# Graph build of a four-layer graph network: count, weight and edge-bias columns from one product of 22 values, and batch sums in two pairs of PSUM banks

## The chip, the cores and the metric

One core of a Trainium2 chip runs the whole program. The metric is the device time of one execution in microseconds, as the median of runs. TensorE (PE in the profile) multiplies matrices, VectorE (DVE) and ScalarE (ACT) do elementwise work, GpSimd (POOL) gathers rows, SyncE (SP) issues most transfers.

## The reference

```
h = relu(layernorm(x));  x = x + attention(h, batch0, edge_index, edge_attr_16, ...)   # 32 graphs of 64 nodes, 8 heads
h = relu(layernorm(x));  x = x + gcn3(h, edge_index, ...)                              # normalised by in-degrees
h = relu(layernorm(x));  x = x + gcn1(h, edge_index, ...)                              # normalised by out-degrees
h = relu(layernorm(x));  x = x + relu(segment_sum((h @ W)[col] * edge_weight, row))
```

x has 2048 rows of 512. The 67584 edges (src, dst, 16 attributes, a weight) are sorted by dst. The kernel turns them once into dense matrices: `count` (how many edges between two nodes), the weights' sums (the last layer's matrix) and, for edges inside one graph of attention, the edge biases `edge_attr @ We + be` summed by pair of nodes. That work is the build. All later layers are dense products with these matrices.

## The kernel before

**Edge preparation** (to 50 us) finds where each node's edges begin and writes records of 11 fields to DRAM: src, dst, weight, 8 biases.

**The build** (50 to 419 us) handles edges in units of 64 partitions: one half of the partitions holds the edges of one destination node, the other half those of another. A tile is 128 such units; there are 8 tiles (t), each in 8 batches of 16 units, so 64 batches (n, with i = n modulo 8). For a tile, GpSimd gathers the records, TensorE turns them (`turn_fields`, L1154), ScalarE copies the fields to SBUF (`copy_fields`, L980), and VectorE makes keys (`prep_keys`, L779 to L790): the low 7 bits of src, and the tile of src. Values are split into two fp16 parts: ScalarE writes the high ones (`copy_part`, L991 for weights, L992 for biases), VectorE the rest (`residual`, L810, L811).

For a batch, `hots` on VectorE writes into one of two buffers: a comparison for counts and weights (L872, 32 columns per unit), one for the biases (L875, 16 columns twice), the one-hot rows of src (L877, 128 columns), the count columns times the weight parts (L887) and the tile columns times the bias parts (L894, 256 columns). It needs batch n-2 to be through TensorE. TensorE then (`build_pe`) sums the biases over the batch in one bank (L1255, 32 matmuls), and counts and weights of each unit in its own columns of four banks (L1266, L1267, 16 pairs). ScalarE copies both out (`copy_sums`: L1006 biases, L1013 counts, L1020 weights to a slab). TensorE turns the slab of batch n-4 (L1166), ScalarE scales it (L1001) and SyncE stores it.

**What runs beside it.** In the same batches the attention's projections are computed: TensorE turns h (L1175), ScalarE casts it to `h_t` (L1033), VectorE subtracts to get the low part (L819, inside `hots`, before the product), TensorE projects (L1201 in fp32 for the first slab, L1209, L1192), ScalarE copies results to `stage` (L1070, L1073, L1076) and SyncE stores them. `projections` fixes in which batch each piece stands: h is turned at batches 1, 6, 12, 17, 22, 28 and 33.

**Order and banks.** Each engine runs its own program in written order; semaphores join them. Turned fields, h pieces, projections and turned slabs share a ring of three PSUM banks (`work_slots`); a use waits until the third use before it has been read. In-degrees are one small matmul per tile (L1264) into spare columns of the sums' banks, added by VectorE in `evacuate` (L905), which waits for the slab copy.

In each ScalarE iteration n the order is: the batch's stage copies and casts, `copy_sums`, the scaled slab, and where i is 3 `copy_part` of the next tile.

## Time and profile before

| what | us |
|---|---|
| median of 3 runs | 1401.82 |
| lowest, highest | 1401.14, 1402.6 |
| span of the profiled execution | 1400.5 |
| PE, DVE, ACT busy in it | 1363.9, 886.7, 568.6 |

The profile comes from one execution. Its span runs from the first to the last instruction, without what lies around it. "Busy" of an engine is the time in which at least one of its instructions ran; matmuls are pipelined, so a row of 32 shows the last one's whole length after the start of the first. A start-to-start distance is therefore the better price of one instruction in a queue than its duration. `[1.96 <-DVE x_sb L894]` behind a row says that the engine had stood idle for 1.96 us and what ended it. Tile names come without buffer numbers; all one-hot columns lie in the memory of `x_sb`, all PSUM banks are `banks`.

### The profile page before, as it was taken

Reading aid. Unit: us, or ns where it says so; the run is one execution under the profiler, and the core shown is the slowest. Engines: PE = TensorE matmul, PEld = TensorE weight load, DVE = VectorE, ACT = ScalarE, POOL = GpSimd, SP = SyncE. Lnnn points to the kernel's source line nnn. Section 1 sums busy time; section 2 is a strip of 40 time slices with the busy share of each in tenths; the row PEclk is TensorE's granted clock in tenths of the full one; section 3 lists DMA queues with packets and bytes.
Section 4 is the critical chain, followed back from the end, with each engine's and each line's share of the span. In section 5 each row is a group of like instructions: output and inputs, shape, how many; then the busy total and the mean of one; then the engine's idle time right before and its main releaser. Section 6 shows DMA issues by size and latency. Waiting matters only on the chain.

```text
span 1400.5 us, 26694 instructions
## 1 busy us (share of the span) xinstructions
PE 1363.9 (97%) x11285; PEld 843.1 (60%) x11285; DVE 886.7 (63%) x1381; ACT 568.6 (41%) x980; POOL 88.0 (6%) x86
## 2 busy tenths in 40 slices
PE   9889999989998999999999999999999999999998
PEld 8779898989996655544444444454444445344443
DVE  7998998999988886567555666542354223532323
ACT  2666566656554457411142113221253224422312
POOL 3120010101002110000001000011100000000000
PEclk9999999999999999999999999999999999999999
DMA  9634344335348723000002000022210222563201
GB/s 335 227 114 148 137 138 137 126 119 177 120 146 286 238 94 108 1 31 1 0 0 61 0 0 1 1 59 77 68 40 29 73 71 78 200 212 104 91 0 60
DMA packets 71333, 136.92 MB, mean 98 GB/s; under 512 B 11908, under 2 KB 24324, under 8 KB 69798
## 3 DMA queue, kind: packets, MB, share of 16 engines
q1 hardware_dynamic: 68542, 123.98, 26.8%
q0 software_dynamic: 1280, 5.77, 1.5%
q10 hardware_dynamic: 1384, 5.38, 1.1%
q8 instruction: 92, 1.51, 0.5%
q14 instruction: 35, 0.29, 0.1%
HBM read 81.79 MB, written 53.32 MB: 96 GB/s over the span
## 4 chain that ended last, share of the span: by engine, by line
PE 83%; DVE 11%; ACT 2%; issue 2%; DMA 1%; POOL 0%; ACTq 0%; SPq 0%; DVEq 0%; POOLq 0%
PE banks L2305 31%; PE banks L2239 13%; PE banks L2369 12%; PE banks L1255 6%; PE banks L1655 4%; DVE x_sb L894 3%; PE banks L1192 3%; PE banks L1209 2%; PE banks L1266 2%; PE banks L1166 2%; DVE x_sb L877 1%; PE banks L2183 1%; PE banks L1625 1%; PE banks L298 1%; PE banks L1643 1%
## 5 line engine op out<-in xcount | busy, mean ns | idle before, releaser
L2305 PE MATMUL banks<-g,count 128*128 128x512 f16 x1024 | 227.6, 379 | 0.5 <-DVE tiles L2571 0.5
L2305 PE MATMUL banks<-count,g 128*128 128x512 f16 x1024 | 223.6, 379 | 0.0
L2239 PE MATMUL banks<-w_parts,h_parts 128*128 128x512 f16 x960 | 215.3, 379 | 1.7 <-DVE g L2520 1.4
L2305 PEld LDWEIGHTS banks<-count,g 128*128 128x128 f16 x1024 | 99.6, 98 | 118.0
L2305 PEld LDWEIGHTS banks<-g,count 128*128 128x128 f16 x1024 | 99.7, 98 | 113.6 <-DVE tiles L2571 1.0
L2369 PE MATMUL banks<-g,part 128*128 128x512 f16 x768 | 165.9, 379 | 0.0
L2239 PEld LDWEIGHTS banks<-w_parts,h_parts 128*128 128x128 f16 x960 | 91.2, 98 | 115.4 <-issue 11.4
L894 DVE TENSOR_TENSOR x_sb<-eb_parts,x_sb 128x4096 f16<-128x4096 f16 x64 | 146.0, 2281 | 0.0
L1255 PE MATMUL banks<-x_sb 128*128 128x128 f16 x2048 | 126.9, 221 | 11.9 <-DVE x_sb L894 11.8
L1255 PEld LDWEIGHTS banks<-x_sb 128*128 128x128 f16 x2048 | 120.9, 99 | 15.3 <-DVE x_sb L894 14.2
L2369 PEld LDWEIGHTS banks<-g,part 128*128 128x128 f16 x768 | 75.1, 98 | 90.6
L2652 DVE SCALAR_TENSOR_TENSOR part<-count,e_scale,part 128x1024 f16<-128x1024 f32 x29 | 37.2, 1284 | 105.9 <-ACT part L2136 105.9
L2110 ACT ACTIVATE h_gcn_t<-h_gcn_t,b_col,unscale 128x512 f32<-128x512 f32 x32 | 26.0, 813 | 169.2 <-DVE h_gcn_t L2563 169.2
L2136 ACT ACTIVATE part<-count,e_scale 128x1024 f16<-128x1024 f32 x29 | 33.3, 1148 | 110.9 <-PE banks L2369 110.9
L877 DVE TENSOR_TENSOR x_sb<-iota_src,keys 128x2048 f16<-128x2048 f16 x64 | 77.7, 1215 | 0.0
L2459 DVE TENSOR_TENSOR h_parts<-h_gcn_t,h_parts 128x512 f16<-128x512 f32 x48 | 39.6, 829 | 48.6 <-ACT h_parts L2019 48.6
L1266 PE MATMUL banks<-x_sb 128*128 128x64 f16 x1024 | 65.1, 190 | 0.0
L1267 PE MATMUL banks<-x_sb 128*128 128x32 f16 x1024 | 64.2, 178 | 0.0
L2520 DVE SCALAR_TENSOR_TENSOR g<-banks,g_scale,g 128x512 f16<-128x512 f32 x64 | 47.6, 747 | 22.1 <-ACT g L2042 22.0
L1266 PEld LDWEIGHTS banks<-x_sb 128*128 128x128 f16 x1024 | 60.8, 97 | 0.5
L1655 PE MATMUL banks<-wo_sb,att_t 128*128 128x512 f32 x128 | 58.7, 602 | 0.4 <-ACT att_t L1563 0.4
L1267 PEld LDWEIGHTS banks<-x_sb 128*128 128x128 f16 x1024 | 59.0, 96 | 0.1
(346 smaller groups left out, 1902.5 us busy)
## 6 DMA issues: line engine op xcount, KB each, us to landing
weight_dram<-w_new SPq DMA_DIRECT2D x60, 256.0 KB, 2.6
count<-weight_dram SPq DMA_DIRECT2D x29, 512.0 KB, 7.1
qk_dram<-stage SPq DMA_DIRECT2D x64, 128.0 KB, 2.6
tiles<-x_dram SPq DMA_DIRECT2D x32, 256.0 KB, 3.5
x_dram<-tiles SPq DMA_DIRECT2D x32, 256.0 KB, 2.8
count<-in_x SPq DMA_DIRECT2D x4, 1024.0 KB, 12.8
h<-in_x SPq DMA_DIRECT2D x16, 256.0 KB, 4.3
h_dram<-h_t SPq DMA_DIRECT2D x8, 512.0 KB, 3.3
```

Source lines behind the costliest of these rows:

```text
L877: dve.tensor_tensor(m.hot_src[:, z].rearrange("p g (c two) -> p g c two", two=2), keep.iota_src[:].rearrange("p (c two) -> p c two", two=2 ...
L894: dve.tensor_tensor(m.hot_eb[:, z].rearrange("p g (t c) -> p g t c", t=NT), values, tiles, ALU.mult).then_inc(s["hots"], 1)
L1192: mm = pe.matmul(out, m.h_slab[slab % 2][:, zh, k, tile * P:(tile + 1) * P], keep.wq[:, zw, k, c * SCOLS:(c + 1) * SCOLS], start=n == 0, s ...
L1255: mm = pe.matmul(m.bias_ps[:, 0:NT * H], m.hot_src[:, z, g], parts[:, part], start=g == part == 0, stop=g == BATCH - 1 and part == 1)
L1266: pe.matmul(m.cw_ps[:, g, 0:2 * CCOLS], m.hot_src[:, z, g], m.hot_cw[:, z, g, 0:2 * CCOLS], start=True, stop=False)
L1267: mm = pe.matmul(m.cw_ps[:, g, CCOLS:2 * CCOLS], m.hot_src[:, z, g], m.hot_cw[:, z, g, 2 * CCOLS:CW], start=False, stop=True)
L1655: mm = pe.matmul(m.wo_ps[:, t % 2], m.att_t[:, k, :], keep.wo[:, k, :], start=k == 0, stop=k == KT - 1)
L2239: mm = pe.matmul(out, m.h_parts[:, slot, zh, k], m.w_parts[:, zw, k], start=n == 0 and layer != 3, stop=n == len(passes) - 1)
L2305: mm = pe.matmul(m.agg_ps[:, b], lhs, rhs, start=i == 0 and z == 0, stop=i == NT - 1 and z == 1)
L2369: mm = pe.matmul(m.banks[:, b], m.part[:, n % 3, z, b * P:(b + 1) * P], m.g[:, q, gz], start=q == 0 and (z, gz) == (0, 0), stop=q == NT - ...
L2459: dve.tensor_tensor(out, source, hi, ALU.subtract).then_inc(s["lo"], 1)
L2520: dve.scalar_tensor_tensor(lo, result, scale, hi, ALU.mult, ALU.subtract).then_inc(s["glo"], 1)
```

## The change

A unit now has one row of 22 values in fp16: 8 high bias parts, 8 low ones, the weight's low part for each half of the partitions, its high part for each half, and a one for each half (zero in the other half). One comparison makes 16 tile columns twice (L873 after the change), and one product (L889) multiplies all 11 pairs of values with these 32 contiguous columns, 352 columns per unit in place of 256 plus 64. The comparison L872 and the product L887 are gone. The zeros and ones are written before the first keys (`mark_halves`); the weight times its scale, zero in the other half, is made with the keys into `w_half`. `copy_part` stands one batch later and waits for the keys. The sums of counts and weights take 64 columns per unit, so a batch fills two banks, and two batches alternate between two pairs. The in-degree matmul takes a bank of the ring.

```diff
@@ -564 @@ build_memory
-    n_src, n_eb, n_cw, n_tile = (2 * BATCH * c for c in (P, NT * HP, CW, 2 * NT))
-    m.eb_parts = place("eb_parts", [P, 2, P, HP], F16, AT_EB)
+    n_src, n_val, n_tile = (2 * BATCH * c for c in (P, NT * VALUES, 2 * NT))
+    m.parts = place("parts0", [P, P, VALUES], F16, AT_EB)[:], place("parts1", [P, P, VALUES], F16, AT_REST + 15360)[:]
     m.w_slab = place("w_slab", [P, 2, 4, BATCH * CCOLS], F32, AT_SLAB)
     m.fields = place("fields", [P, FIELDS, P], F32, AT_REST + 5632)
     m.h_t = place("h0_t", [P, 2, KT, SCOLS], F16, AT_REST + 11264)
-    m.keys = place("keys", [P, 2, 2, P, 2], BF16, AT_REST + 15360)
-    m.ints = place("ints", [P, 3, P], I32, AT_REST + 17408)
-    m.w_parts = place("w_parts", [P, 2, P, 2, 2], F16, AT_REST + 18944)
+    m.ints = place("ints", [P, 2, P], I32, AT_EB + 5632)
+    m.w_half = m.ints[:].rearrange("p two u -> p (two u)").bitcast(F32).rearrange("p (u half) -> p u half", half=2)
+    m.src_keys = [place(f"src_key{z}", [P, P, 2], BF16, AT_EB + 6656 + 512 * z)[:] for z in range(2)]
+    m.tile_keys = place("tile_key0", [P, P, 2], BF16, AT_EB + 7680)[:], place("tile_key1", [P, P, 2], BF16, AT_REST + 23040)[:]
...
-    m.cw_ps = keep.banks[:, WORK:7].rearrange("p b (g c) -> p (b g) c", c=P)
-    m.deg_ps = m.cw_ps[0:2 * GTILES, 0:GROUPS, CW:P]
+    m.cw_ps = keep.banks[:, WORK:7].rearrange("p (z b) (g c) -> p z (b g) c", z=2, c=2 * CCOLS)
@@ -716 @@ work_slots
+        if i == 0:
+            use(("deg", t), ("added", t + 1 if first_round else n + 1))
@@ -780 @@ prep_keys
-        dve.tensor_scalar(m.ints[:, 1], m.ints[:, 0], P - 1, None, ALU.bitwise_and)
-        dve.tensor_scalar(m.ints[:, 2], m.ints[:, 0], 7, None, ALU.logical_shift_right).then_inc(s["dve"], 1)
+        dve.tensor_scalar(m.ints[:, 1], m.ints[:, 0], P - 1, None, ALU.bitwise_and).then_inc(s["dve"], 1)
+        k += 1
+        dve.wait_ge(s["dve"], k)
+        dve.tensor_scalar(m.ints[:, 0], m.ints[:, 0], 7, None, ALU.logical_shift_right).then_inc(s["dve"], 1)
         k += 1
         dve.wait_ge(s["dve"], k)
         dve.tensor_scalar(keep.match[:], dlocal, 0.0, None, ALU.is_equal)
         twice = [P, P, 2]
-        dve.tensor_copy(m.keys[:, z, 0], m.ints[:, 1].unsqueeze(2).to_broadcast(twice))
-        dve.scalar_tensor_tensor(m.keys[:, z, 1], dlocal.unsqueeze(2).to_broadcast(twice), float(P),
-                                 m.ints[:, 2].unsqueeze(2).to_broadcast(twice), ALU.mult, ALU.add).then_inc(s["keyed"], 1)
+        dve.tensor_copy(m.src_keys[z], m.ints[:, 1].unsqueeze(2).to_broadcast(twice))
+        settle(dve.scalar_tensor_tensor(m.tile_keys[z], dlocal.unsqueeze(2).to_broadcast(twice), float(P),
+                                 m.ints[:, 0].unsqueeze(2).to_broadcast(twice), ALU.mult, ALU.add))
+        dve.tensor_tensor(m.w_half, m.fields[:, 2, :].unsqueeze(2).to_broadcast(twice),
+                          keep.half_scale[:].unsqueeze(1).to_broadcast(twice), ALU.mult).then_inc(s["keyed"], 1)
@@ -804 @@ residual
-        dve.scalar_tensor_tensor(m.w_parts[:, z, units, 1], weight, keep.scale[:, 1:2], m.w_parts[:, z, units, 0], ALU.mult, ALU.subtract)
-        dve.scalar_tensor_tensor(m.eb_parts[:, z, units, H:HP], biases, keep.scale[:, 0:1], m.eb_parts[:, z, units, 0:H],
+        dve.tensor_tensor(parts[:, units, W_LO:W_LO + 2], m.w_half[:, units], parts[:, units, W_HI:W_HI + 2], ALU.subtract)
+        dve.scalar_tensor_tensor(parts[:, units, H:HP], biases, keep.scale[:, 0:1], parts[:, units, 0:H],
@@ -861 @@ hots
-        dve.tensor_tensor(cw[:, :, 0:CCOLS].rearrange("p g (c two) -> p g c two", two=2),
-                          keep.iota_cnt[:].rearrange("p (c two) -> p c two", two=2).unsqueeze(1).to_broadcast([P, BATCH, NT, 2]),
-                          key(1, CCOLS), ALU.is_equal).then_inc(s["dve"], 1)
-        dve.tensor_tensor(m.hot_tile[:, z], keep.iota_tile[:].unsqueeze(1).to_broadcast([P, BATCH, NT, 2]),
-                          m.keys[:, ts, 1, units].unsqueeze(2).to_broadcast([P, BATCH, NT, 2]), ALU.is_equal).then_inc(s["dve"], 1)
+        dve.tensor_tensor(m.hot_tile[:, z].rearrange("p g (t two) -> p g t two", two=2), keep.iota_tile[:].unsqueeze(1).to_broadcast([P, BATCH, NT, 2]),
+                          m.tile_keys[ts][:, units].unsqueeze(2).to_broadcast([P, BATCH, NT, 2]), ALU.is_equal).then_inc(s["dve"], 1)
         dve.tensor_tensor(m.hot_src[:, z].rearrange("p g (c two) -> p g c two", two=2),
                           keep.iota_src[:].rearrange("p (c two) -> p c two", two=2).unsqueeze(1).to_broadcast([P, BATCH, P // 2, 2]),
-                          key(0, P), ALU.is_equal)
+                          m.src_keys[ts][:, units].unsqueeze(2).to_broadcast([P, BATCH, P // 2, 2]), ALU.is_equal)
         nonlocal k
-        k += 2
+        k += 1
         dve.wait_ge(s["dve"], k)
         if n == 0:
             residual(0)
         if units.start in [u.start for u in unit_parts(t, first_round)]:
             dve.wait_ge(s["parts"], part_count(t, 1 if units.start else 0, first_round))
-        dve.tensor_tensor(cw[:, :, CCOLS:CW].rearrange("p g (z c two) -> p g z c two", z=2, two=2),
-                          cw[:, :, 0:CCOLS].rearrange("p g (c two) -> p g c two", two=2).unsqueeze(2).to_broadcast([P, BATCH, 2, NT, 2]),
-                          m.w_parts[:, ts, units].unsqueeze(3).to_broadcast([P, BATCH, 2, NT, 2]), ALU.mult)
         for tile in turned:
             h_low(tile)
-        tiles = m.hot_tile[:, z].rearrange("p g t two -> p (g t) two").unsqueeze(2).to_broadcast([P, BATCH * NT, H, 2])
-        values = m.eb_parts[:, ts, units].unsqueeze(2).to_broadcast([P, BATCH, NT, HP])
-        dve.tensor_tensor(m.hot_eb[:, z].rearrange("p g (t c) -> p g t c", t=NT), values, tiles, ALU.mult).then_inc(s["hots"], 1)
+        tiles = m.hot_tile[:, z].unsqueeze(2).to_broadcast([P, BATCH, PAIRS, 2 * NT])
+        values = m.parts[ts][:, units].rearrange("p u (c two) -> p (u c) two", two=2).unsqueeze(2).to_broadcast([P, BATCH * PAIRS, NT, 2])
+        dve.tensor_tensor(m.hot_val[:, z].rearrange("p g (c t) -> p g c t", c=PAIRS), values, tiles, ALU.mult).then_inc(s["hots"], 1)

+    def mark_halves():
+
+        for parts in m.parts:
+            settle(dve.memset(parts[:, :, HP:VALUES], 0.0))
+            for half in range(2):
+                dve.memset(parts[half * WHALF:(half + 1) * WHALF, :, ONE + half], 1.0)
+        if first_round:
+            dve.wait_ge(keep.prep["pool"], 12)
+            dve.tensor_scalar(keep.half_scale[:], keep.half_of[:, GTILES - 1:2 * GTILES:GTILES], keep.scale[:, 1:2], None, ALU.mult)
@@ -896 @@ evacuate
-            dve.wait_ge(s["slab"], n + 1)
-            part = CPT // GROUPS
-            op = dve.tensor_tensor(keep.deg[:].rearrange("q b (g c) -> q b g c", c=part), m.deg_ps.rearrange("q g (c b) -> q b g c", c=part),
-                                   keep.deg[:].rearrange("q b (g c) -> q b g c", c=part), ALU.add)
+            bank, _ = uses["deg", n // NBATCH]
+            dve.wait_ge(s["batch"], n + 1)
+            op = dve.tensor_tensor(keep.deg[:], m.work_ps[0:2 * GTILES, bank, 0:P].rearrange("q (c b) -> q b c", c=CPT), keep.deg[:], ALU.add)
@@ -930 @@ build_dve
     pieces = projections(first_round)
+    mark_halves()
     if first_round:
         other_norms()
     prep_keys(0)
@@ -983 @@ copy_part
-        act.activation(m.w_parts[:, z, units, 0], weight, ACT.Copy, scale=keep.scale[:, 1:2])
-        act.activation(m.eb_parts[:, z, units, 0:H], biases, ACT.Copy, scale=keep.scale[:, 0:1]).then_inc(s["copied"], 1)
+        act.wait_ge(s["keyed"], t + 1)
+        act.copy(parts[:, units, W_HI:W_HI + 2], m.w_half[:, units])
+        act.activation(parts[:, units, 0:H], biases, ACT.Copy, scale=keep.scale[:, 0:1]).then_inc(s["copied"], 1)
@@ -1003 @@ copy_sums
-            act.copy(to_count, m.cw_ps[:, :, 0:CCOLS].rearrange("p (c b) (h s) -> p s c b h", c=GROUPS, h=2))
+            act.copy(to_count, sums[:, :, CCOLS:2 * CCOLS].rearrange("p (c b) (s h) -> p s c b h", c=GROUPS, h=2))
...
-        slab = m.w_slab[:, q % 2, n % 4].rearrange("p (b c) -> p b c", b=BATCH)
-        act.copy(slab, m.cw_ps[:, :, CCOLS:2 * CCOLS]).then_inc(s["slab"], 1)
+        slab = m.w_slab[:, q % 2, n % 4].rearrange("p (b h s) -> p b h s", h=2, s=NT)
+        act.copy(slab, sums[:, :, 0:CCOLS].rearrange("p b (s h) -> p b h s", h=2)).then_inc(s["slab"], 1)
@@ -1121 @@ build_act
-        if t + 1 < GTILES and i == 3:
+        if t + 1 < GTILES and i == 4:
             copy_part(t + 1)
@@ -1250 @@ build_pe
-            parts = m.hot_eb[:, z, g].rearrange("p (t two h) -> p two t h", two=2, h=H)
             for part in range(2):
-                mm = pe.matmul(m.bias_ps[:, 0:NT * H], m.hot_src[:, z, g], parts[:, part], start=g == part == 0,
+                mm = pe.matmul(m.bias_ps[:, 0:EB_COLS], m.hot_src[:, z, g], m.hot_val[:, z, g, part * EB_COLS:(part + 1) * EB_COLS], start=g == part == 0,
                                stop=g == BATCH - 1 and part == 1)
         mm.then_inc(s["bias_done"], 1)
         if t + 1 < GTILES and i == 3:
             turn_fields(t + 1)
-        if n:
-            pe.wait_ge(s["slab"], n)
-            pe.wait_ge(s["added"], added(n - 1))
+        if n >= 2:
+            pe.wait_ge(s["slab"], n - 1)
+            if not first_round:
+                pe.wait_ge(s["added"], n - 1)
         if i == 0:
-            pe.matmul(m.deg_ps, keep.half_of[:, GTILES - 1 - t:3 * GTILES - 1 - t], keep.match[:], start=True, stop=True)
+            bank, free = uses["deg", t]
+            if free:
+                pe.wait_ge(s[free[0]], free[1])
+            pe.matmul(m.work_ps[0:2 * GTILES, bank, 0:P], keep.half_of[:, GTILES - 1 - t:3 * GTILES - 1 - t], keep.match[:], start=True, stop=True)
         for g in range(BATCH):
-            pe.matmul(m.cw_ps[:, g, 0:2 * CCOLS], m.hot_src[:, z, g], m.hot_cw[:, z, g, 0:2 * CCOLS], start=True, stop=False)
-            mm = pe.matmul(m.cw_ps[:, g, CCOLS:2 * CCOLS], m.hot_src[:, z, g], m.hot_cw[:, z, g, 2 * CCOLS:CW], start=False, stop=True)
+            pe.matmul(m.cw_ps[:, z, g], m.hot_src[:, z, g], m.hot_val[:, z, g, W_HI * NT:VALUES * NT], start=True, stop=False)
+            mm = pe.matmul(m.cw_ps[:, z, g, 0:CCOLS], m.hot_src[:, z, g], m.hot_val[:, z, g, W_LO * NT:W_HI * NT], start=False, stop=True)
```

ScalarE, from batch 11 to the projections of batch 13. Before:

```order
L1020 COPY w_slab<-banks 128x512
L1001 ACTIVATE w_new<-banks,scale 128x512 [waits first_store1,first_chunk]
L991 ACTIVATE w_parts<-fields,scale 128x128x2 [waits first_hots,first_turned]
L992 ACTIVATE eb_parts<-fields,scale 128x128x8
L1073 ACTIVATE stage<-banks,bk_col,w_small 128x256 [waits first_out_p3,first_proj]
L1033 CAST h_t<-banks 128x4x128 [waits first_out_h,first_h_turned] x2
L1006 COPY bias<-banks 128x16x8 [waits first_bias_done]
L1013 CAST count<-banks 128x64x8 [waits first_batch]
```

And after, from the same place on:

```order
L1032 COPY w_slab<-banks 128x512
L1012 ACTIVATE w_new<-banks,scale 128x512 [waits first_store1,first_chunk]
L1085 ACTIVATE stage<-banks,bk_col,w_small 128x256 [waits first_out_p3,first_proj]
L1045 CAST h_t<-banks 128x4x128 [waits first_out_h,first_h_turned] x2
L1017 COPY bias<-banks 128x128 [waits first_bias_done]
L1025 CAST count<-banks 128x64x8 [waits first_batch]
L1032 COPY w_slab<-banks 128x512 [waits first_chunk]
L1012 ACTIVATE w_new<-banks,scale 128x512 [waits first_store0,first_chunk]
L1002 CAST parts_79<-ints 128x128x2 [waits first_keyed,first_hots,first_turned]
L1003 ACTIVATE parts_79<-fields,scale 128x128x8
L1082 ACTIVATE stage<-banks,bq_col,w_small 128x256 [waits first_out_p0,first_proj]
```

The two value copies moved behind the casts of h and behind batch 12's sums, and the first of them waits for the keys.

VectorE at the start of the build (`parts_79` and `parts_80` are the two value tiles). Before:

```order
L523 TENSOR_SCALAR scale<-scale 128x4 [waits prep_dve]
L1421 TENSOR_LOAD rounds [waits counted]
L798 RECIPROCAL rstd<-rstd 128x12 [waits prep_std]
L801 SCALAR_TENSOR_TENSOR shift<-stats_119,rstd 128x12 [waits first_dve]
L779 CAST ints<-fields 128x128 [waits first_turned]
```

After:

```order
L521 TENSOR_SCALAR scale<-scale 128x4 [waits prep_dve]
L1435 TENSOR_LOAD rounds [waits counted]
L894 MEMSET parts_79 128x128x3
L896 MEMSET parts_79 64x128 [waits first_dve]
L896 MEMSET parts_79 64x128
L894 MEMSET parts_80 128x128x3
L896 MEMSET parts_80 64x128 [waits first_dve]
L896 MEMSET parts_80 64x128
L899 TENSOR_SCALAR half_scale<-half_of,scale 128x2 [waits prep_pool]
L804 RECIPROCAL rstd<-rstd 128x12 [waits prep_std]
L807 SCALAR_TENSOR_TENSOR shift<-stats_122,rstd 128x12 [waits first_dve]
L781 CAST ints<-fields 128x128 [waits first_turned]
```

Seven instructions stand ahead of the norms and the first keys that did not stand there.

## Rows read from the trace of the kernel before

**Rows 1.** The page's first part: busy us, share of span, instructions.
```profile
PE 1363.9 (97%) x11285; PEld 843.1 (60%) x11285; DVE 886.7 (63%) x1381; ACT 568.6 (41%) x980; POOL 88.0 (6%) x86
```
**Rows 2.** Busy time by stretch: length, PE, PEld, DVE, ACT, POOL, granted clock, DMA share, GB/s.
```profile
100.00:145.00 45.00, 42.43 (x685) 40.05 (x683) 40.59 (x52) 29.55 (x59) 2.94 (x2) 1.00 0.49 156
```
**Rows 3.** Waits of PE in 50-180, 180-300, 300-420: us, times, longest.
```profile
PE banks L1255 <- DVE x_sb L894: 5.8, 4, 2.0
...
PE banks L1255 <- DVE x_sb L894: 4.9, 2, 2.9
...
PE banks L1255 <- DVE x_sb L894: 1.2, 1, 1.2
```
**Rows 4.** Timeline of DVE, one batch: start, duration, line, tiles, count, [idle before].
```profile
110.16 0.43 DVE L872 TENSOR_TENSOR x_sb<-iota_cnt,keys 128x512 f16<-128x512 f16 x1
...
110.83 1.23 DVE L877 TENSOR_TENSOR x_sb<-iota_src,keys 128x2048 f16<-128x2048 f16 x1
111.97 0.70 DVE L887 TENSOR_TENSOR x_sb<-x_sb,w_parts 128x1024 f16<-128x1024 f16 x1
112.57 2.29 DVE L894 TENSOR_TENSOR x_sb<-eb_parts,x_sb 128x4096 f16<-128x4096 f16 x1
115.74 0.28 DVE L905 TENSOR_TENSOR deg<-banks,deg 16x128 f32<-16x128 f32 x1 [0.87 <-ACT w_slab L1020]
```
**Rows 5.** Timeline of DVE at the program's start: a memset.
```profile
0.94 0.27 DVE L424 MEMSET bins<- 128x256 f32 x1 [0.94 <-PEq L2801]
```
**Rows 6.** Timelines of DVE, ACT and PE at the start of the build.
```profile
50.48 0.23 DVE L779 CAST ints<-fields 128x128 int32<-128x128 f32 x1 [0.28 <-ACT fields L980]
...
51.41 0.35 ACT L991 ACTIVATE w_parts<-fields,scale 128x64 f16<-128x64 f32 x1
...
54.17 0.82 ACT L1070 ACTIVATE stage<-banks,bq_col 128x256 f32<-128x256 f32 x2
...
55.78 3.62 PE L1201 MATMUL banks<-h_first,w_slab 128*128 128x256 f32 x16
...
59.65 1.95 PE L1255 MATMUL banks<-x_sb 128*128 128x128 f16 x32
```
**Rows 7.** Timeline of DVE in the keys of a tile.
```profile
139.72 0.22 DVE L784 TENSOR_SCALAR ints<-ints 128x128 int32<-128x128 int32 x1
139.98 0.23 DVE L787 TENSOR_SCALAR match<-fields 128x128 f16<-128x128 f32 x1
...
140.32 0.42 DVE L790 SCALAR_TENSOR_TENSOR keys<-fields,ints 128x256 bf16<-128x256 f32 x1
```
**Rows 8.** Timeline of PE at batch 7's bias product.
```profile
105.70 1.51 PE L1255 MATMUL banks<-x_sb 128*128 128x128 f16 x24 [0.64 <-DVE x_sb L894]
```
**Rows 9.** Timelines of DVE, ACT and PE, batches 12 to 15.
```profile
130.84 0.42 DVE L872 TENSOR_TENSOR x_sb<-iota_cnt,keys 128x512 f16<-128x512 f16 x1 [1.00 <-PE banks L1267]
...
132.78 2.11 ACT L992 ACTIVATE eb_parts<-fields,scale 128x1024 f16<-128x1024 f32 x1
...
135.85 1.29 DVE L819 TENSOR_TENSOR h_t<-banks,h_t 128x512 f16<-128x512 f32 x2 [2.51 <-ACT h_t L1033]
...
152.34 1.85 PE L1255 MATMUL banks<-x_sb 128*128 128x128 f16 x30 [1.96 <-DVE x_sb L894]
```
**Rows 10.** Timelines of ACT and PE, batches 20 to 23.
```profile
185.93 0.70 ACT L1001 ACTIVATE w_new<-banks,scale 128x512 f32<-128x512 f32 x1
...
193.10 1.06 ACT L1033 CAST h_t<-banks 128x512 f16<-128x512 f32 x2
...
198.07 0.34 PE L1255 MATMUL banks<-x_sb 128*128 128x128 f16 x3
```
**Rows 11.** PE after a wait: its row, then stretches (length, busy, granted clock, DMA).
```profile
244.70 1.51 PE L1255 MATMUL banks<-x_sb 128*128 128x128 f16 x24 [1.96 <-DVE x_sb L894]
...
246.00:248.00 2.00, 2.00 (x40) 0.52 0.00 0
248.00:250.00 2.00, 2.00 (x21) 0.63 0.00 0
```

49 lines of the change are left out of this document (25 added, 24 removed).

## The prediction

> **What bounds the kernel now.** I read in this order: busy time by engine, the build in stretches, who waited for whom, then single rows. TensorE is busy for 1363.9 of 1400.5 us [rows 1]. The change touches the build alone, 64 batches between about 50 and 419 us. There VectorE is nearly as full, 40.59 of 45 us against TensorE's 42.43 between 100 and 145 us [rows 2]. Two chains run side by side, tied by two buffers of one-hot columns. The waits say which is late: TensorE's bias product waited for VectorE's value product L894 for 5.8 us before 180, 4.9 until 300, 1.2 after [rows 3]. Nothing on TensorE waited for the batch sums to be copied (no row names L1266). So VectorE sets the pace in the first 55 us of the build and in short stretches later, TensorE elsewhere. VectorE time moves the end only on those stretches, and 11.9 us of such waits is all that there is.
>
> **The VectorE batch.** From start to start L872 and L875 take 0.67 us together, L877 1.14, L887 0.60; L894 lasts 2.29, of which 0.09 overlaps the next, so 4.61 a batch [rows 4]. L872 (0.34) and L887 go: -0.94. L894 grows from 4096 to 5632 columns. Its slope comes from two rows of one form: 2048 columns take 1.22 us, 4096 take 2.29, so 0.522 ns a column, and 1536 more are 0.80 us. Net -0.14 us a batch, 9 us in all, most of it where TensorE is late anyway. The new product repeats a pair of columns 16 times against 32 contiguous ones; L877 too repeats a pair against a contiguous row, and runs at L894's slope, so I take that slope. The other end is one column a cycle, as in fp32: L790's 256 columns in 0.42 us [rows 7], 0.15 of it fixed (1.22 less 2048x0.522), are 1.05 ns a column, +3 us a batch. The Trainium skill, "Advanced Engine Details and Errata", section 2x-1p Requirements, asks 16-bit types, a 4-byte aligned start and unit step innermost for two elements a cycle; rows of 22 values, 44 bytes, keep that, so by the page too the fast form stands.
>
> **TensorE's own work** I cost at nothing. The bias products lose a strided operand. 32 of them take 1.95 us [rows 6]; with a tail of 0.2 that is 56 ns each for 128 columns, 2.7 ns over the 53.3 of the full clock. If that were all the stride, 2048 of them would give 5.5 us back. I take none, since every row of matmuls has some such excess; it is a reason for the low end. The sums keep 64 and 32 columns per unit. The second pair of banks relaxes a wait that is in no row: nothing.
>
> **Start (+1.8).** VectorE now clears and marks both value tiles right before the first keys. A clear is 384 words wide; 256 words took 0.27 us [rows 5], 0.05 of it overlap, so 0.33, plus 0.1 for the wait on it (L784 to L787, across a wait, is 0.26; L787 to L790, two starts without one, 0.34 [rows 7], so 0.17 each). Four marks of 128 are 0.12 each, the scaling 0.15: 1.5 us, of which 0.28 fits in the wait that L779 had [rows 6]: +1.2. The keys get two waits (0.1 each) and a product of 256 columns in fp32 like L790 (0.34 to the next start): 0.54, with its rounding taken as +0.6 per tile of eight batches. ScalarE's first copy waits for those keys (51.41 before, 53.9 after), and with it its queue: the stage copies at 54.17. TensorE's fourth projection needs the first stage copy's bank, at 57.2 instead of 55.8; bias 0 goes from 59.65 to about 61.5 [rows 6]. VectorE ends batch 1's columns 1.5 us late (1.2+0.6-2x0.14) and has no idle time before 115 us: -0.14 for each of six batches, +0.6 for the second tile's keys, +0.5 for a cast of h that ScalarE delivers late at batch 6, since its value copy now stands behind the keys. +1.8 at the bias product of 105.70 [rows 8]. From there TensorE is late by itself and carries that on. Ends: +0.5 if ScalarE's lateness stays hidden and the marks are cheaper, +3.5 if it is not.
>
> **The value copy one batch later.** L991 and L992 hold ScalarE 2.4 us once a tile (the larger is 2.11 [rows 9]), after batch 3 of the tile; now after batch 4 and behind the keys. Take T as the moment when VectorE begins the columns of batch 5 of a tile: 130.84 after 1.00 us of waiting for TensorE [rows 9], and so in four more tiles, at 179.16, 223.21, 272.10 and 317.24. Keys are ready at T+4.47+2.0=T+6.5; ScalarE is at that place of its queue at T+7.5 where two projections precede (185.93 and 0.6 more [rows 10]), so it mostly doesn't wait and ends at T+10. TensorE needs its banks at T+12. Nothing is lost there.
> Two tiles win, batches 12 and 28 (T=130.84 and 223.21), where h is turned at batch 4 of the tile. Before, the casts stood behind the value copy: VectorE waited 2.51 us for them, until T+5.0, and TensorE at the end 1.96 us for VectorE [rows 9]. Now the casts end at T+3.5, both subtractions T+4.1, the product (3.0) T+7.1, keys T+9.1, batch 6's columns (4.47) T+13.6, residuals (2.3) T+15.9, batch 7's columns T+20.4, and its bias product starts at T+20.5 instead of T+21.5 (152.34). TensorE alone would be there at T+19.4. So -1.0 each, -2.0 for both, not 2.5 each, since VectorE stays the late one.
> One tile loses, batch 22 (T=179.16). ScalarE's value copy ends at T+9.9; then come two stage copies, two relus, the copies of batch 21 (their bank free at T+14.25), one stage copy and the casts, which end at T+16.3 instead of T+15.0 (193.10 and 1.06). VectorE's subtractions, then the product, put the bias product of batch 23 at T+19.6 instead of T+18.9 (198.07 [rows 10]): +0.7. The tile at 272 turns no h there; its keys cost +0.6 and three batches give back 0.4: +0.2.
>
> **The in-degree count** moves to the ring of three work banks. VectorE's wait for it was for the slab copy (0.87 us at 115.74 [rows 4]) and is now for the batch itself, about 1.1 us earlier; VectorE runs into TensorE again at the next T in every tile, so nothing. The ring's next user of that bank comes after the next batch's bias product, where the old wait stood too: nothing.
>
> **Sum.** +1.8 -2.0 +0.7 +0.2 = +0.7 on a span of 1400.5: 1401.2. The median of the runs, 1401.82, is 1.3 above that span; the same on top gives **1402.5 us**.
>
> **Rivals.** *The clock.* After the 1.96 us wait at 244.70 TensorE's granted clock read 0.52 and 0.63 for two times 2 us [rows 11], so for about 1.7 us the work of full clock (2.4 GHz) was withheld at half of it; the equal wait at 152.34 left it at full. I price that at 1.5. With the wait halved the drop may go: 1402.5-1.5=1401.0, still no change; with a start at its low end (-1.3) and no loss at batch 22 (-0.7) it is 1399.0, at the edge of faster. The Trainium skill, "TensorE: Matmul & The Clock Gate", section What's actually happening, says that the activity window runs free of the kernel; by that a shift of 1.8 us alone could place or remove a drop, which fits that equal waits ended differently here. *ScalarE becomes the late engine (slower).* Place: behind the keys at batch 4 of each tile. TensorE's turns of h at batch 6 need a bank that ScalarE frees after the value copy, three copies later; there I get 2.4 us of new wait, counted as covered because VectorE is late too. It decides where the value copy ends later than T+12, that is, if keys or copies are 2 us slower than taken. Then the start costs 3.5, batch 22 2.0, the two gains fall to 0.5 each, and one new drop of the clock comes on top (1.5): 1401.8+3.5-1.0+2.0+0.2+1.5=1408. *The product loses the fast form:* 64 times 3 us, about 1590. *VectorE's saving counts everywhere (faster):* the start costs nothing, both gains stand, and the waits [rows 3] shrink by 0.14 for each of some 20 batches ahead of them: 1401.8-2.0-2.8=1397.
>
> **Chances.** A measurement of this kernel can tell about 0.2%, 2.8 us. The forecast has 0.48, the clock's 1401.0 another 0.14, its edge and VectorE's saving everywhere 0.17, ScalarE late 0.18, the slow product 0.03. So faster 0.17, same 0.62, slower 0.21. Range: 1397.8 to 1406.5; it reaches most of the way to both rivals and leaves out the slow product.
>
> **What would show it.** The new product at 3.05 to 3.15 us; batch starts 4.47 us apart where VectorE is full; first keys near 51.8 and bias 0 near 61.5; the 2.5 us wait for the casts at batches 12 and 28 down to about 1.5; a wait of ScalarE for keys of 2 us in the first tile, little later; TensorE's waits for the product no fewer than before in the first 60 us. Wrong would be: a product off 3.1 us, ScalarE copies over 0.7 us because their source in PSUM is now strided, bias products under 55 ns, or a second tile in which TensorE waits for ScalarE.

## The result and the profile after

The changed kernel takes **1403.65 us** (median of 20 runs, 1402.18 to 1405.15) against 1401.81 (20 runs on the same chips): a ratio of 1.0016, 95% interval 1.001 to 1.0022. That is within 0.2% and inside the range; the point, 1402.5, was 1.15 low. Its profiled execution spans 1402.1 us, 1.6 more than before. The kernel before scatters from 1399 to 1404 and the medians of single experiments are good to about 1 us, so below I follow each effect in the traces and name the median beside it.

Busy time first, the page's first part (busy us, share of span, instructions), which answers [rows 1]:

```profile
PE 1364.0 (97%) x11285; PEld 841.3 (60%) x11285; DVE 883.6 (63%) x1268; ACT 568.6 (41%) x980; POOL 85.6 (6%) x84
```

VectorE has 113 instructions fewer and is busy for only 3.1 us less, and none of that is seen at the end. TensorE's waits for the value product, by the groups of PE in the three stretches 50 to 180, 180 to 300, 300 to 420 (count, busy, mean ns, idle before them and for whom), against [rows 3]:

```profile
L1265 PE MATMUL banks<-x_sb 128*128 128x128 f16 x640 | 39.0, 219 | 3.6 <-DVE x_sb L889 2.7 <-ACT bias L1017 0.9
...
L1265 PE MATMUL banks<-x_sb 128*128 128x128 f16 x675 | 42.2, 222 | 4.2 <-DVE x_sb L889 4.2
...
L1265 PE MATMUL banks<-x_sb 128*128 128x128 f16 x736 | 44.9, 219 | 1.0 <-DVE x_sb L889 1.0
```

These waits fell from 11.9 to 7.9 us, and yet the kernel is no faster. To see where the time went, take the start of the bias product of each batch after (L1265) less the same before (L1255). This offset is +4.4 us at batch 0, +4.2 at batches 7 to 12, +3.25 at batches 15 to 21, +3.6 at 23 to 28, +2.7 at 31, +1.3 at 32 to 37, +1.1 from 41 to the last; the rest of the 1.6 comes behind the build. So against this trace everything is lost in the first 5 us of the build and most of it won back later. VectorE's timeline there (start, duration, line, tiles, count, [idle before]), against [rows 6]:

```profile
49.81 0.17 DVE L521 TENSOR_SCALAR scale<-scale 128x4 int32<-128x4 int32 x1
50.53 0.38 DVE L894 MEMSET parts<- 128x384 uint32 x1 [0.55 <-issue]
51.43 0.17 DVE L896 MEMSET parts<- 64x128 f16 x1 [0.53 <-DVE parts L894]
52.11 0.17 DVE L896 MEMSET parts<- 64x128 f16 x1 [0.51 <-issue]
52.40 0.38 DVE L894 MEMSET parts<- 128x384 uint32 x1
53.30 0.17 DVE L896 MEMSET parts<- 64x128 f16 x1 [0.52 <-DVE parts L894]
53.97 0.17 DVE L896 MEMSET parts<- 64x128 f16 x1 [0.51 <-issue]
54.15 0.23 DVE L899 TENSOR_SCALAR half_scale<-half_of,scale 128x2 f32<-128x2 f16 x1
...
54.63 0.22 DVE L781 CAST ints<-fields 128x128 int32<-128x128 f32 x1
```

A mark (L896, a fill of one column with 1.0) is busy for 0.17 us, but 0.51 to 0.53 us of idle time stand before each of the four. From the first clear to the start of the scaling it is 3.6 us where I had 1.5 with the scaling in it. The last step of the scaling factor, L521 here and L523 before, also starts 0.65 later (49.81 against 49.16), ahead of all that the change touches; I call this the drift and take it off: 4.20 - 0.65 = **3.55 us** is what the start costs against this one trace of the kernel before. That trace is an early one: four more profiles below have the start of the kernel before unchanged (the two with the later copy alone and two built on it), and their offsets at batch 2 are 0.3, 1.2, 1.2 and 2.1. The drift explains this only in part (it is 0.3, -0.55, 1.1 and 0.6); the section on the hardware comes back to it.

The places of the two gains, VectorE's subtraction of h at batch 12 and TensorE's bias products of batches 15, 23 and 31, against [rows 9 to 11]:

```profile
138.04 1.29 DVE L824 TENSOR_TENSOR h_t<-banks,h_t 128x512 f16<-128x512 f32 x2 [1.44 <-ACT h_t L1045]
...
155.59 1.62 PE L1265 MATMUL banks<-x_sb 128*128 128x128 f16 x26 [0.90 <-DVE x_sb L889]
...
201.68 1.51 PE L1265 MATMUL banks<-x_sb 128*128 128x128 f16 x24 [0.17 <-DVE x_sb L889]
...
247.37 1.85 PE L1265 MATMUL banks<-x_sb 128*128 128x128 f16 x30 [0.90 <-DVE x_sb L889]
```

VectorE's wait for the casts is 1.44 instead of 2.51, TensorE's two waits 0.90 instead of 1.96. And TensorE's clock after the wait at 247.37 (length, busy of each engine, granted clock, DMA share, GB/s):

```profile
248.00:250.00 2.00, 2.00 (x55) 2.00 (x53) 2.00 (x2) 0.39 (x1) 0.00 (x0) 1.00 0.21 66
250.00:252.00 2.00, 2.00 (x26) 1.84 (x22) 2.00 (x2) 1.67 (x3) 0.00 (x0) 1.00 0.00 0
```

It stays at full clock (2.4 GHz) where [rows 11] read 0.52 and 0.63. The offset falls by 1.39 us between batches 31 and 32: that is this drop's price.

The single product and the keys, grouped over the build's VectorE work (count, busy us, mean ns, idle before):

```profile
L889 DVE TENSOR_TENSOR x_sb<-parts,x_sb 128x5632 f16<-128x5632 f16 x64 | 197.2, 3081 | 0.0
...
L796 DVE TENSOR_TENSOR ints<-fields,half_scale 128x256 f32<-128x256 f32 x8 | 3.4, 424 | 0.3
```

### The profile page after: what moved, and what is told of

Its sections match the earlier page's. It is cut to its first block, busy times and chain, and to the rows that moved or that the text cites. A ratio compares the mean times of both kernels' runs of the same rounds, so it can differ in the third digit from the quotient of the medians.

```text
span 1402.1 us, 26531 instructions
## 1 busy us (share of the span) xinstructions
PE 1364.0 (97%) x11285; PEld 841.3 (60%) x11285; DVE 883.6 (63%) x1268; ACT 568.6 (41%) x980; POOL 85.6 (6%) x84
## 4 chain that ended last, share of the span: by engine, by line
PE 83%; DVE 12%; ACT 2%; issue 2%; DMA 1%; DVEq 0%; ACTq 0%
PE banks L2319 31%; PE banks L2253 13%; PE banks L2383 11%; PE banks L1265 6%; DVE x_sb L889 5%; PE banks L1669 3%; PE banks L1206 3%; PE banks L1223 2%; PE banks L1280 2%; PE banks L1180 2%; DVE x_sb L875 1%; PE banks L2197 1%; PE banks L1639 1%; PE banks L296 1%; PE banks L1657 1%
## 5 line engine op out<-in xcount | busy, mean ns | idle before, releaser
L889 DVE TENSOR_TENSOR x_sb<-parts,x_sb 128x5632 f16<-128x5632 f16 x64 | 197.2, 3081 | 0.0
L2253 PEld LDWEIGHTS banks<-w_parts,h_parts 128*128 128x128 f16 x960 | 91.1, 98 | 115.1 <-issue 11.9
L1265 PE MATMUL banks<-x_sb 128*128 128x128 f16 x2048 | 125.8, 220 | 8.7 <-DVE x_sb L889 7.9
L1265 PEld LDWEIGHTS banks<-x_sb 128*128 128x128 f16 x2048 | 119.9, 98 | 12.2 <-DVE x_sb L889 11.0
L875 DVE TENSOR_TENSOR x_sb<-iota_src,src_key 128x2048 f16<-128x2048 f16 x64 | 77.7, 1215 | 0.0
```

The costliest lines, as they stand in the source:

```text
L875: dve.tensor_tensor(m.hot_src[:, z].rearrange("p g (c two) -> p g c two", two=2), keep.iota_src[:].rearrange("p (c two) -> p c two", two=2 ...
L889: dve.tensor_tensor(m.hot_val[:, z].rearrange("p g (c t) -> p g c t", c=PAIRS), values, tiles, ALU.mult).then_inc(s["hots"], 1)
L1265: mm = pe.matmul(m.bias_ps[:, 0:EB_COLS], m.hot_src[:, z, g], m.hot_val[:, z, g, part * EB_COLS:(part + 1) * EB_COLS], start=g == part == ...
L2253: mm = pe.matmul(out, m.h_parts[:, slot, zh, k], m.w_parts[:, zw, k], start=n == 0 and layer != 3, stop=n == len(passes) - 1)
```

## The experiments

Theory A: the change loses its time in the marks at the start, gains by the later value copy (with the clock), and the single product itself saves nothing. Rivals: ScalarE, held up behind the keys, is what is late at the start (B); the clock moves by itself (C).

### The later copy alone, on the kernel before

```diff
-        if t + 1 < GTILES and i == 3:
+        if t + 1 < GTILES and i == 4:
             copy_part(t + 1)
```

> The kernel before, with only ScalarE's value copy (L991 and L992) moved from behind batch 3 of a tile to behind batch 4; two products, the count comparison and the old banks stay. Theory A (the change's gains come from the moved copy, its losses from the marks and keys at the start): batches 12 and 28 gain 1.5 each (VectorE's wait for the casts of h goes from 2.5 to about 1.0 us), the drop of the clock at 244.70 goes too (1.4), batch 22 loses 0.3, the start is unchanged: 1401.8 - 3.0 - 1.4 + 0.3 = 1397.7, ratio 0.997. Theory B (the copy is neutral, and what the changed kernel gained there came from the shorter VectorE batch): within 0.5 of 1401.8. Theory C (the clock's drop came away by the shift of the time alone, free of the wait): 1401.8 - 2.7 = 1399.1 with 0.5 for two stretches of 2 us still in the clock's row near 246.

Measured: **1395.87 us** (5 runs, 1395.67 to 1396.24), ratio 0.9958, interval 0.9944 to 0.9971. It is ahead of both kernels, clear of the scatter. At batch 12 and at batch 15's bias product:

```profile
134.10 1.29 DVE L819 TENSOR_TENSOR h_t<-banks,h_t 128x512 f16<-128x512 f32 x2 [0.43 <-ACT h_t L1033]
...
150.58 0.62 PE L1255 MATMUL banks<-x_sb 128*128 128x128 f16 x8 [0.59 <-DVE x_sb L894]
```

The wait for the casts went from 2.51 to 0.43. Against the kernel before, the offset falls by 2.09 at batch 12 and 2.11 at batch 28, not 1.5: 1.37 each is TensorE's wait before the last product of the tile, and 0.72 I had not seen, a wait of TensorE's projections for VectorE's subtraction (0.56 us at 137.28 before) that goes as well. The drop at 246 goes (1.39), and so does the one at 290, for 0.95 more. These are 6.5; less a drift of 0.3 and 0.1 lost at batch 22, the last batch comes 6.1 earlier. Here is the clock from the end of TensorE's wait of 2.96 us, at 285.34, on:

```profile
284.00:286.00 2.00, 0.66 (x12) 0.66 (x13) 2.00 (x3) 0.00 (x0) 0.00 (x0) 1.00 0.05 17
286.00:288.00 2.00, 2.00 (x56) 2.00 (x54) 2.00 (x4) 0.38 (x1) 0.00 (x0) 1.00 0.27 37
```

Theory A holds in kind and was too low in size; the neutral copy is out. That the clock goes by itself is not excluded by this one kernel, in which both waits and times changed.

> The same kernel as the one before with the value copy behind batch 4, once more, for the clock. Its first profile had a wait of 2.96 us of TensorE at 285 and no drop, where the kernel before had 2.94 and a drop. If the program's own waits decide on the drop, this one is again without drops in the build, and the time within 0.5 of 1395.9. If it is the time at which the wait falls against something free of the kernel, drops may come in the build in one of the runs, and with each about 1.4 us: up to 1398.7.

The same kernel once more: 1397.0 us (5 runs, 1395.41 to 1398.24), ratio 0.9962, interval 0.9949 to 0.9975. Its profile again has no drop between batch 0 and the end of the build, and every wait for the product repeats within 0.05 us. But its bias 0 is 0.97 us later than in the first profile and all that follows 0.9, with the same program and a scaling factor that is ready 0.8 earlier: TensorE's clock came back to full at 52.2 instead of 48.8. One of the five runs, at 1398.24, is high enough to hold a drop; the spread does not say where.

### The later copy undone, in the changed kernel

First the order alone: ScalarE copies the bias fields ahead of its wait for the keys.

```diff
-        act.wait_ge(s["keyed"], t + 1)
-        act.copy(parts[:, units, W_HI:W_HI + 2], m.w_half[:, units])
-        act.activation(parts[:, units, 0:H], biases, ACT.Copy, scale=keep.scale[:, 0:1]).then_inc(s["copied"], 1)
+        act.activation(parts[:, units, 0:H], biases, ACT.Copy, scale=keep.scale[:, 0:1])
...
+    def copy_weight(t, piece=0):
...
+        act.wait_ge(s["keyed"], t + 1)
+        act.copy(parts[:, units, W_HI:W_HI + 2], m.w_half[:, units]).then_inc(s["copied"], 1)
...
+            copy_weight(t + 1)
```

> The changed kernel, with ScalarE's value copy (bias fields, L1003) issued ahead of the wait for the keys and only the small copy of the weights (L1002) behind it; same places in the queue. In the first tile ScalarE waits 3.99 us for the keys, and 2.63, 2.3 and 1.1 us later. Theory A (VectorE's marks and keys are what is late; ScalarE follows): VectorE's residual starts at most 0.6 us earlier and the stage copies 2.3 us earlier, TensorE's wait of 1.69 us for the stage copy goes, and bias 0 moves by 0.5: 1403.65 - 0.5 = 1403.1. Rival (ScalarE held up behind the keys is the late engine): 2 us or more off the start and 1 more at the second tile: 1400.6.

Measured: 1403.54 us (11 runs, 1402.03 to 1404.16), no change from 1403.65. ScalarE did get ahead: TensorE's projection at the start waited 0.89 for the stage copy instead of 1.69, and without the drifts bias 0 came 1.85 earlier, not the 0.5 that I expected. But then TensorE waited for VectorE and had lost all of it by batch 1, first for w_small, then for the in-degrees' bank:

```profile
68.23 1.99 PE L1222 MATMUL banks<-h_first,w_slab 128*128 128x256 f32 x8 [0.77 <-DVE w_small L846]
71.27 1.09 PE L1196 MATMUL banks<-ident,h 128*128 128x128 f32 x8 [1.04 <-DVE deg L916]
```

At batch 7 the offset less its own drift (L521 at 50.16, so 1.0) is 3.57, against 3.55 with ScalarE behind the keys. So ScalarE's 4 us of waiting cost nothing at the end; theory B is out, and my -0.5 with it.

Then the bias fields' copy back behind batch 3 (`i == 3`), with the small copy of the weights still behind batch 4:

> The changed kernel, with the bias fields' copy (L1003) back behind batch 3 of a tile as before the change, and only the small copy of the weights behind the keys after batch 4. It undoes the move by one batch. Theory A (the move gave 0.95 at each of batches 12 and 28 and 1.4 by the clock): against the version that only swaps the two copies 1.9 lost plus up to 1.4: 1403.1 + 2.6 = 1405.7, with VectorE's wait for the casts of h back at 2.5 us. Rival (the move is neutral): 1403.1 and that wait at 1.4.

Measured: 1408.93 us (5 runs, 1408.13 to 1410.83), 5.4 above the version with the order alone; I had said 2.6.

```profile
139.19 1.29 DVE L824 TENSOR_TENSOR h_t<-banks,h_t 128x512 f16<-128x512 f32 x2 [3.11 <-ACT h_t L1049]
...
156.73 1.46 PE L1273 MATMUL banks<-x_sb 128*128 128x128 f16 x23 [2.05 <-DVE x_sb L889]
```

The wait for the casts is 3.11. From trace to trace the move is worth 1.68 at each of batches 12 and 28 and 1.39 by the clock, 4.75 together. The error was in taking 0.95 for the move: 0.95 is what was left of it after the rest of the change had taken its part. With the copy early, the changed kernel is **0.7 behind the kernel before** at each of the two batches (offset 3.68 before batch 12 and 4.39 from batch 15 on).

### The marks

Two copies out of a constant tile in place of two clears and four marks:

```diff
-        for parts in m.parts:
-            settle(dve.memset(parts[:, :, HP:VALUES], 0.0))
-            for half in range(2):
-                dve.memset(parts[half * WHALF:(half + 1) * WHALF, :, ONE + half], 1.0)
         if first_round:
             dve.wait_ge(keep.prep["pool"], 12)
+        for parts in m.parts:
+            settle(dve.tensor_copy(parts[:, :, ONE:VALUES], keep.half_of[:, GTILES - 1:2 * GTILES:GTILES].unsqueeze(1).to_broadcast([P, P, 2])))
...
```

> The changed kernel, with the two clears and four marks of mark_halves (3.6 us of VectorE from the first to the last) replaced by two copies of 256 columns out of half_of, about 0.35 us each. Theory A: first keys 2.9 us earlier (51.8 instead of 54.6), bias 0 and all that follows 2.5 to 2.9 earlier, since VectorE has no idle time until 115 us: 1403.65 - 2.7 = 1401.0. Rival (the late start is TensorE's and ScalarE's own, the marks hide behind them): bias 0 moves by less than 1 us and the total by less than 0.7: 1403.0.

Measured: 1401.4 us (11 runs, 1399.35 to 1402.62), 2.25 less than the changed kernel.

```profile
49.49 0.63 DVE L896 COPY parts<-half_of 128x256 f16<-128x256 f16 x2 [0.43 <-issue]
...
50.71 0.23 DVE L781 CAST ints<-fields 128x128 int32<-128x128 f32 x1
...
58.85 1.22 DVE L830 TENSOR_TENSOR h_t<-h_first,h_t 128x1024 f16<-128x1024 f32 x1 [0.63 <-ACT h_t L1115]
```

The start costs 1.30 now (offset 1.03 at batch 7, drift -0.27) instead of 3.55: the clears and marks are 2.25 of it, by trace and by median alike. VectorE's keys are 3.0 earlier when each drift is taken off; 0.63 of that VectorE gives back in a wait for h that it did not have. Theory A, 0.4 off in size.

The reverse, the same clears and marks put into the kernel before, ahead of the first keys:

```diff
...
+        for z in range(2):
+            parts = m.hot_eb[:, z].rearrange("p g c -> p (g c)")[:, 0:22 * P].rearrange("p (u c) -> p u c", c=22)
+            settle(dve.memset(parts[:, :, 16:22], 0.0))
+            for half in range(2):
+                dve.memset(parts[half * WHALF:(half + 1) * WHALF, :, 20 + half], 1.0)
```

> The kernel before, with nothing changed but two clears and four marks of the changed kernel's shapes added ahead of the first keys (into the one-hot columns' memory, which the first batch overwrites). Theory A (the marks are the larger part of the late start, and nothing downstream gives them back): they take 3.6 us of VectorE as in the changed kernel, 0.28 fits in a wait, TensorE's own chain covers about 0.7 more: bias 0 2.6 later, 1401.9 + 2.6 = 1404.5. Rival (as I had sized them: 1.5 us less 0.28): 1403.1. Rival (hidden): 1402.0.

Measured: 1404.02 us (12 runs, 1402.76 to 1405.66), ratio 1.0018, interval 1.0009 to 1.0027. That is 2.4 above the kernel before on the same chip, nearer to the 2.6 of theory A than to the 1.2 that I had sized first. The six fills take as long as in the changed kernel. Bias 0 is only 2.56 later; at batch 2 TensorE waits 3.21 us for VectorE's product, and from there to batch 31 the offset is 4.32, 3.48 without its drift of 0.84. So the whole start cost of the changed kernel by the same reckoning (3.55) is there with nothing changed but the marks. The last batch comes only 2.7 later, since the drop at 246 is missing from this trace too:

```profile
249.03 1.18 PE L1268 MATMUL banks<-x_sb 128*128 128x128 f16 x18 [1.95 <-DVE x_sb L894]
...
250.00:252.00 2.00, 2.00 (x52) 2.00 (x50) 2.00 (x3) 0.50 (x2) 0.00 (x0) 1.00 0.00 0
252.00:254.00 2.00, 2.00 (x21) 1.80 (x20) 2.00 (x3) 1.80 (x4) 0.00 (x0) 1.00 0.00 0
```

This is the same wait as in [rows 11], 1.95 against 1.96 us, and no drop. So a halved wait is not needed to lose the drop. What differs here is the time at which the wait falls; that this is the cause is not shown.

What makes a mark dear? 14 small fills and copies in front of the first keys of the kernel before:

```diff
+        for half in range(2):
+            dve.memset(parts[half * WHALF:(half + 1) * WHALF, :, 2 + half], 0.0)
+        for j in range(2):
+            dve.memset(parts[:, :, 4 + j], 1.0)
+        for j in range(2):
+            dve.memset(parts[:, :, 6 + j], 0.0)
...
+        for j in range(2):
+            dve.memset(flat[:, 128 * j:128 * j + 128], 1.0)
...
```

> The kernel before, with 14 small operations of VectorE ahead of the first keys: clears and fills of 128 columns strided by 22 on 64 and on 128 partitions with 0.0 and with 1.0, fills of pairs, fills of 128 contiguous columns, copies of a pair and of one column from half_of. In the changed kernel each fill of 1.0 on 64 partitions had 0.51 to 0.53 us of idle time before it, and one of two wide clears 0.55. If the value 1.0 causes it, the fills of 1.0 on 128 partitions and the contiguous ones show it and the clears don't; if 64 partitions cause it, the clears and copies on 64 partitions show it and none on 128; if the stride causes it, all but the contiguous ones show it; if it is any fill, copies alone are without it. The time is some 4 to 8 us above the kernel before.

It took 1407.27 us (one run). VectorE's timeline, in order: single columns on 64 partitions with 0.0, on 128 with 1.0, on 128 with 0.0; then pairs of columns with 1.0 (two), contiguous ones (two), copies of pairs (two), copies of single columns on 64 partitions (two):

```profile
51.57 0.17 DVE L945 MEMSET x_sb<- 64x128 f16 x1 [0.51 <-issue]
52.25 0.17 DVE L947 MEMSET x_sb<- 128x128 f16 x1 [0.51 <-issue]
52.82 0.17 DVE L947 MEMSET x_sb<- 128x128 f16 x1 [0.41 <-issue]
53.39 0.17 DVE L949 MEMSET x_sb<- 128x128 f16 x1 [0.41 <-issue]
53.97 0.17 DVE L949 MEMSET x_sb<- 128x128 f16 x1 [0.41 <-issue]
54.12 0.55 DVE L951 MEMSET x_sb<- 128x256 f16 x2
54.64 0.30 DVE L953 MEMSET x_sb<- 128x128 f16 x2
54.87 0.63 DVE L955 COPY x_sb<-half_of 128x256 f16<-128x256 f16 x2
55.42 0.75 DVE L957 COPY x_sb<-half_of 64x128 f16<-64x128 f16 x2
```

Neither the value nor the number of partitions matters much: every fill of single 16-bit elements at a stride of 44 bytes has 0.4 to 0.5 us before it, fills of pairs and of contiguous columns have none. Twice as many elements in pairs are done in 0.27 us each, less than half the time of the single ones. The idle time is not a tail of the fill before: the first fill of pairs starts 0.15 us after the last single one, with none, and in the changed kernel so do the second clear and the scaling behind a mark. It goes with the single fill that follows it. Nor is the stride alone enough: the two copies of single 16-bit columns have no idle time and take 0.75 us together. The dear form is a fill of single 16-bit elements; what the engine does in that time the records can't say.

Last, the same 128 places as one 32-bit word each:

```diff
-            settle(dve.memset(parts[:, :, HP:VALUES], 0.0))
+            words = parts.rearrange("p u c -> p (u c)").bitcast(I32).rearrange("p (u w) -> p u w", w=PAIRS)[:, :, ONE // 2]
             for half in range(2):
-                dve.memset(parts[half * WHALF:(half + 1) * WHALF, :, ONE + half], 1.0)
+                op = dve.memset(words[half * WHALF:(half + 1) * WHALF], 15360 << 16 * half)
+            settle(op)
```

> The changed kernel, with the two wide clears left out (their other columns are written anyway) and each of the four marks written as one 32-bit word per unit (one half 1.0, the other 0.0) in place of one 16-bit column: the same 64 partitions, the same 128 places 44 bytes apart. In the probe, fills of single 16-bit columns had 0.41 to 0.51 us of idle time before each, whatever the value and the partitions, fills of pairs and of contiguous columns none. Theory D (it is the lone 16-bit element): marks 0.15 each without idle time, with one wait on them 0.8 us in all instead of 3.6, VectorE's first keys 2.8 earlier than in the changed kernel against the end of the scaling chain, 2.2 kept at the end as with the copied marks: 1401.4. Rival (it is the lone element of any size, at a stride): about 0.5 idle before each, 2.7 us in all, and 1402.8.

```profile
50.28 0.17 DVE L896 MEMSET parts<- 64x128 int32 x1 [0.58 <-issue]
50.61 0.17 DVE L896 MEMSET parts<- 64x128 int32 x1 [0.17 <-issue]
50.96 0.17 DVE L896 MEMSET parts<- 64x128 int32 x1 [0.19 <-DVE parts L896]
51.28 0.17 DVE L896 MEMSET parts<- 64x128 int32 x1 [0.16 <-issue]
```

1401.16 us (11 runs, 1398.58 to 1402.6), 0.2 from what was expected. 0.33 us from one to the next instead of 0.68: mostly the 16-bit element. Against the end of the scaling chain the keys come 2.4 earlier, not 2.8, and the offset without drift is 1.32 at batch 7, so 2.2 are kept, as with the copied marks (the two wide clears are gone here too). The idle time of 0.16 to 0.19 that is left was not expected with it, so theory D is right in the main and not in full. Some idle time before the first operation (0.58) stands in all these versions of the changed kernel (0.55, 0.43).

### The single product

> The kernel before with the value copy behind batch 4 (1395.9 us) and one more edit: where h is turned, the weights' product L887 (0.60 from start to start) stands behind VectorE's subtractions for h instead of ahead of them, so that it no longer runs while VectorE would wait for the casts. It is a model of what the single product does, which holds the weights' part too and comes as a whole behind the casts. Theory A (the single product lengthens what stands between the casts and the bias product): batches 12 and 28 lose 0.6 each, and 22 up to 0.6, so 1397.3 to 1397.7. Rival (it costs nothing, since VectorE catches up): within 0.4 of 1395.9.

```diff
+        for tile in turned:
+            h_low(tile)
         dve.tensor_tensor(cw[:, :, CCOLS:CW].rearrange("p g (z c two) -> p g z c two", z=2, two=2),
                           cw[:, :, 0:CCOLS].rearrange("p g (c two) -> p g c two", two=2).unsqueeze(2).to_broadcast([P, BATCH, 2, NT, 2]),
                           m.w_parts[:, ts, units].unsqueeze(3).to_broadcast([P, BATCH, 2, NT, 2]), ALU.mult)
-        for tile in turned:
-            h_low(tile)
```

Measured: 1398.92 us (11 runs, 1397.85 to 1401.3), more than the 1397.3 to 1397.7 expected and 3.0 and 1.9 above the two sets of runs of the same kernel with L887 ahead. At batches 12 and 15:

```profile
135.06 1.29 DVE L819 TENSOR_TENSOR h_t<-banks,h_t 128x512 f16<-128x512 f32 x2 [1.10 <-ACT h_t L1033]
...
152.15 1.07 PE L1255 MATMUL banks<-x_sb 128*128 128x128 f16 x16 [1.28 <-DVE x_sb L894]
```

VectorE waits 0.67 longer for the casts, since it has 0.6 less to do meanwhile, and TensorE waits 1.28 instead of 0.59. The offset grows by 0.69 at batch 12, 0.49 at 22 and 0.70 at 28, 1.9 in all; 0.95 more comes with the clock, whose drop at 290 is back. So work that stood in a wait and is moved behind it costs its full length. The single product does just this with the weights' part of itself; that it pays for it in the same way is argued from this model and fits the 0.7 a batch by which the changed kernel with the early copy is behind.

Two versions more make the price of the product's surroundings visible. In both, the product of weights and halves (L796) is gone, and the high and low weight columns are each written in two operations of one column per unit:

```diff
...
-        act.wait_ge(s["keyed"], t + 1)
-        act.copy(parts[:, units, W_HI:W_HI + 2], m.w_half[:, units])
+        for half in range(2):
+            act.activation(parts[:, units, W_HI + half], m.fields[:, 2, units], ACT.Copy, scale=keep.half_scale[:, half:half + 1])
```

> The version with the copied marks, in which the product of weights and halves (L796, 0.42 us of VectorE per tile) is gone: ScalarE makes the two high weight columns itself with a scale per partition, two operations of 128 columns in place of one of 256, VectorE subtracts them in two operations in place of one, and ScalarE's value copy no longer waits for the keys. Theory A (VectorE's work per tile counts where VectorE is late; ScalarE's wait hardly): start 0.4 earlier, batches 12 and 28 0.3 each: 1401.4 - 1.0 = 1400.4. Rival (ScalarE behind the keys is what costs): 2 us or more: 1399.2 or less.

Measured: 1402.45 us (12 runs, 1399.79 to 1404.93), 1.05 more than the version with copied marks, where 1.0 less was expected. The two were measured on different chips, and 1.05 is about what such medians are good to; the traces say more clearly that it lost (its last batch is 1.8 later, drifts taken off). ScalarE and then VectorE in one tile of this version, then ScalarE in the one with copied marks:

```profile
139.00 1.47 ACT L1001 ACTIVATE parts<-fields,half_scale 128x128 f16<-128x128 f32 x2
139.93 2.11 ACT L1002 ACTIVATE parts<-fields,scale 128x1024 f16<-128x1024 f32 x1
...
145.29 1.36 DVE L814 SCALAR_TENSOR_TENSOR parts<-fields,half_scale,parts 128x128 f16<-128x128 f32 x2
146.25 2.06 DVE L816 SCALAR_TENSOR_TENSOR parts<-fields,scale,parts 128x1024 f16<-128x1024 f32 x1
```
```profile
141.24 0.43 ACT L1001 CAST parts<-ints 128x256 f16<-128x256 f32 x1 [2.34 <-DVE ints L796]
141.56 2.14 ACT L1002 ACTIVATE parts<-fields,scale 128x1024 f16<-128x1024 f32 x1
```

The two operations of 128 single 16-bit elements overlap, so their price is the distance to the next start: 0.93 us for both on ScalarE and 0.96 on VectorE, where the one of 256 in pairs takes 0.32 and 0.33 (145.52 to 145.85 on VectorE). That is 0.6 more on each engine, once a tile. On VectorE it eats the 0.45 that leaving out L796 gave, and ScalarE, 0.6 us later, fits the 0.6 more that this trace loses at batch 22. Another 1.0 comes from TensorE's clock, which in this trace is at half for 6.9 us from 288.8 on, where the other has 3.4 us from 288.1. My price, taken from element counts, was wrong; the theory is not touched by it.

Then the same with the value copy at `i == 3` again:

> The same with the value copy back behind batch 3 of a tile: of the change there are then only the single product, the keys' layout and the new banks, with neither the moved copy nor the long marks. Theory A: the moved copy is worth 1.7 at each of batches 12 and 28 and the clock's drop 1.4, so 1400.4 + 4.8 = 1405.2, which is 3 above the kernel before: the single product costs more than it saves. At batches 12 and 28 VectorE works 3.05 us between the casts' arrival and the bias product where it worked 2.29 (the weights' product L887 stood ahead of the casts before), so these two batches come 0.7 later each than before. Rival (the single product saves its 0.14 a batch and more): 1400 or less.

Measured: 1407.6 us (6 runs, 1406.55 to 1409.77), 5.15 above the version before it (4.8 expected), 5.8 above the kernel before (3 expected, short for the same reason as the last). It has neither the later copy nor the dear marks, and nothing of the product's saving shows. But it isn't the product alone: the offset grows by 1.84 and 1.88 at batches 12 and 28, where VectorE waits 4.02 us for the casts. That is 0.9 more than in the changed kernel with the early copy, and ScalarE's two single columns, which stand ahead of the casts here, are 0.93.

### Still later

The kernel before with the value copy at `i == 5` and the residuals at `i == 6` instead of 5:

> The kernel before with the value copy behind batch 5 of a tile and VectorE's residuals behind batch 7's columns instead of batch 6's. If the gain comes from the casts no longer standing behind the copy, batch 4 is late enough, nothing more is to be had: 1395.9 within 0.7. If every batch later that the copy stands takes pressure off ScalarE, another 1 to 2: 1394.5. If the later copy meets the turns of h at batch 6 of a tile (batches 22 and 38), or VectorE waits for it before the last batch of a tile, 1 to 2 more: 1397.5.

Measured: 1399.02 us (12 runs, 1396.18 to 1400.73), 3.1 and 2.0 worse than the two sets of runs behind batch 4: the third case. Batches 12 and 28 gain 2.86 and 2.84 us here, 0.75 more than behind batch 4. But batches 22 to 24 lose 2.4, with waits of 0.64 and 0.96 for the product at 198 and 205 that the other version has not, and the clock's drop at 292 is back, for 6.8 us. Of the three places tried, batch 4 is the best; a place that differs from tile to tile was not tried.

## Why the prediction was right

The sum was +0.7 on the span, and it came out at +1.6, or +0.95 without the drift. That it comes so close is luck: one large term was 1.75 too small, and 1.4 came from a term that stood only in a rival. The terms:

- **Start: +1.8 predicted, +3.55 measured** against this trace of the kernel before. The term that was mis-sized. The step that failed is "Four marks of 128 are 0.12 each": they take 0.68 from one to the next. I had priced a strided column of 16-bit elements by its element count and by rows of wide contiguous operations; no row of before showed that form. Behind a start of the kernel before as late as the latest of its four other profiles it would be some 2 us less; the clears and marks by themselves are 2.25 by trace and median, where they stood in the sum with 1.34. The upper end, +3.5, was met only by chance, as it was worked out for ScalarE's lateness, which costs nothing. The other parts of the step hold: first keys at 51.8 were really at 54.6, and bias 0 at 64.1 instead of 61.5, later by the marks and the drift (61.5 did not follow from its premise either: a bank that is free at 57.2 instead of 55.8 makes 61.1). Keys with their waits take 2.1 us instead of 1.56 (54.63 to 56.73), 0.54 as predicted.
- **The two gains: -2.0 predicted, -1.9 measured** (-0.95 and -0.94). The steps are seen one by one: wait for the casts 1.44 (1.5), TensorE's wait 0.90 (half of 1.96), VectorE still the late one. This was the best part, since it was followed instruction by instruction on both engines. The experiments add that it is the difference of two things: the move alone brings 2.1 a batch in the kernel before, and the rest of the change takes 1.1 of it back.
- **Batch 22: +0.7 predicted, +0.36 measured; tile at 272: +0.2 predicted, -0.15 measured.** Signs half right, both small.
- **The clock: 0 in the forecast, -1.4 measured.** The rival's price of 1.5 was right (1.39), and its event came about. Without it the span would be +3.0, so the forecast needed this rival to pay for the marks. Its reason, the halved wait, is not shown: the kernel before with marks has no drop behind a wait of 1.95.
- **The product:** 3.08 us (3.05 to 3.15), 4.47 us from batch to batch where VectorE is full (109.77 to 114.24). The slow form is out. ScalarE's copies of the sums stay at 0.59 us; bias products at 1.95 per 32, so contiguous operands gave nothing.
- **In-degree count: nothing, as predicted,** though TensorE's turn of h now waits for its bank: 0.2 us here, 1.04 in the version with the changed order.
- **ScalarE late (1408):** its waits for the keys are 3.99 us in the first tile, 2.6 in the second and at most 2.35 later, longer than the 2 us foreseen; changing the order on ScalarE gave nothing. This rival had 0.18 and deserved less.
- **VectorE's saving counts everywhere (1397):** excluded by the changed kernel with the early copy at 1408.93, from which all of the clears and marks (2.25) leave 1406.7, and by the version without either at 1407.6.

What I did not see is that 5.3 to 6 us were to be had from one part of the change alone.

## What to carry to other kernels

Judge the parts of a change one by one: here a move of one ScalarE step was worth 5 to 6 us, and the reorganisation packed with it took all of that back. Work that an engine does while it would wait is free; moved behind the wait, it costs its full length. Price small strided operations from a row of the same element size and stride, by the distance from start to start and not by busy time, and write pairs of 16-bit elements instead of single ones.

## What the runs showed of the hardware

- **Fills of single 16-bit elements at a stride are dear.** 128 of them, 44 bytes apart, cost VectorE 0.57 to 0.68 us a fill from start to start, 0.17 of it shown as busy and the rest as idle time before the fill; as 32-bit words 0.33, as pairs 0.27 for 256. The Trainium skill, "VectorE: DVE Perf Modes", section Zero memsets can be issued as uint32, counts one cycle per element whatever the type; the busy times here go with it (0.17 for 128 of 16 and of 32 bits alike, 0.38 for 384), the time from start to start does not.
- **Computed outputs of single 16-bit elements cost less than that, but more than pairs, on two engines.** As a three-operand subtraction on VectorE 128 of them take 0.48 from start to start and on ScalarE 0.47. The same operations write 256 in pairs in 0.39 and 0.40 in the kernel before (L810 at 145.27, L991 at 132.38). Copies of 128 single elements on 64 partitions, in the probe, take 0.75 us busy for two.
- **Equal waits, different clocks.** Before batch 31's product TensorE waited 1.96, 2.07 and 2.77 us in three kernels and its clock then fell to half (1.2 GHz); in three others it waited 1.94 or 1.95 and it stayed at 2.4. Before batch 15's product waits of 1.73 to 2.73 us in six kernels brought no drop, and one of 1.96 in a seventh, the one with 14 fills and copies, brought one (0.50 from 160 to 162). A wait of 2.96 us at 285 brought none in two profiles of one kernel and one of 3.42 at 297 none in another, while waits of 2.73 to 2.96 near there did in nine others, and 3.44 and 3.60 in two more. The Trainium skill, "TensorE: Matmul & The Clock Gate", section What's actually happening, says that the activity is looked at in windows that do not start with the kernel; these rows agree with that and don't prove it. What decides in a given run stays open.
- **The clock ahead of the build.** In every trace TensorE's clock falls to half at around 40 us, in an idle stretch of 3.7 to 5.5 us, and comes back between 48.1 and 53.9 us: at 48 in the kernel before and at 54 in the changed one, although the change touches nothing until 50, and at 48.8 and 52.2 in two profiles of one kernel:

```profile
50.00:52.00 2.00, 1.99 (x9) 0.50 0.14 38
52.00:54.00 2.00, 2.00 (x7) 0.53 0.92 327
```
```profile
50.00:52.00 2.00, 2.00 (x13) 1.00 0.81 172
52.00:54.00 2.00, 2.00 (x11) 1.00 1.07 408
```

  These are TensorE's rows after, then before. It costs TensorE some 1.6 us in the changed kernel (11 matmuls of L1168 take 2.63 us where 11 of L1154 took 1.61, 24 of L1215 take 6.07 where they took 5.43), hidden behind VectorE's marks: with the changed order of ScalarE the clock is back at 51.1 and the start cost is the same (3.57). Where no marks hide it, it counts. Of the four profiles with the start of the kernel before, those with the clock back at 48.8 and 49.5 are 0.1 us late at batch 2 when the drift is taken off, those with 52.2 and 53.4 are 1.8 and 1.5 late, so it is one part of the scatter of some us between runs of one kernel. So in some executions the marks cost less than 3.5 us, which fits the 2.25 and 2.4 of the medians.
